# A decoder layer on one core: the middle piece's second copy moved to GpSimd, small columns batched, and the attention stage's orders rewritten

## What is computed

```python
# 1: self-attention, 16 heads of 8, rotary embedding on q and k
qkv = x @ w_qkv.T                       # per batch 128 x 384
q, k = rope(q), rope(k)
attn = softmax((q @ k.T) * 8 ** -0.5)   # 16 heads x 128 x 128 per batch
x = layernorm(x + (attn @ v) @ w_out.T + b_out)

# 2: cross layer over ctx: correlation by FFT, top 11 lags over all batches
q, k_, v = x @ Wq + bq, ctx @ Wq + bq, ctx @ Wq + bq      # 8 columns each
corr = real(ifft(fft(q) * conj(fft(k_)))).mean((0, 1))    # needs every batch
W, I = top_k(corr, 11); W = softmax(W)
R = sum(W[i] * roll(v, -I[i])); x = layernorm(x + tile(R) @ Wout + bout)

# 3: mixture of 8 experts, top 2, width 256, then two layer norms
y = mixed_experts(x) + x
x = layernorm(x + gamma * (y - mu) * rsqrt(var + 1e-5) + beta)
```

## Time and profile before

| what | us |
|---|---|
| median of 3 runs | 231.09 (230.35 to 231.51) |
| the profiled execution's own time | 231.02 |
| its span, first to last instruction | 229.2 |
| attention stage, about | 103 of the span |
| one batch in the steady part of that stage | 5.0 |
| TensorE busy | 214.5 |
| VectorE busy | 180.9 |
| ScalarE busy | 142.5 |
| GpSimd busy | 111.2 |

### The profile page before, as it was taken

One profiled execution on the slowest core, in us unless ns is written; L12 is line 12 of the kernel. 1 busy time (PEld: TensorE's weight loads), 2 busy tenths in 40 slices (PEclk: granted clock), 3 DMA queues, 4 the chain that ended last, 5 costly groups with the idle time before them and its releaser, 6 DMA issues.

```text
span 229.2 us, 7213 instructions
## 1 busy us (share of the span) xinstructions
PE 214.5 (94%) x2724; PEld 184.1 (80%) x2724; DVE 180.9 (79%) x622; ACT 142.5 (62%) x248; POOL 111.2 (49%) x219
## 2 busy tenths in 40 slices
PE   7989899999999979999999999999999999999970
PEld 7766677787777667778887999789988999889970
DVE  0588999999899899876755779897798868875885
ACT  2487899999999995674489300991029610596112
POOL 5189879999989995513630400252002600040484
PEclk9999999999999999999999999999999999999997
DMA  5951634665655651420000000001000100001001
GB/s 138 286 134 35 106 59 65 158 135 106 149 122 91 43 92 18 127 74 1 3 0 0 3 0 1 0 4 45 4 0 0 46 3 1 0 4 46 1 16 34
DMA packets 32454, 12.32 MB, mean 54 GB/s; under 512 B 19906, under 2 KB 32290, under 8 KB 32418
## 3 DMA queue, kind: packets, MB, share of 16 engines
q1 hardware_dynamic: 31554, 11.48, 24.1%
q10 hardware_dynamic: 864, 0.36, 0.7%
HBM read 6.33 MB, written 1.05 MB: 32 GB/s over the span
## 4 chain that ended last, share of the span: by engine, by line
PE 79%; DMA 7%; DVE 6%; ACT 3%; issue 2%; SPq 1%; DVEq 0%; ACTq 0%
PE bank L1328 13%; PE scoreT_pair L1328 12%; PE score_pair L1298 11%; PE scoreT_pair L1298 8%; PE bank L1042 6%; PE bank L1046 5%; PE bank L965 4%; PE scoreT_pair L997 4%; PE score_pair L981 3%; DMA qT_all<-mT 2%; PE bank L1003 2%; PE bank L1059 2%; DMA early<-in_ctxT 2%; DMA qT_all<-stack 2%; PE scoreT_pair L945 2%
## 5 line engine op out<-in xcount | busy, mean ns | idle before, releaser
L1385 DVE TENSOR_REDUCE rowmax<-score_pair 128x8 f32<-128x1024 f32 x32 | 39.0, 1218 | 4.4 <-PE score_pair L981 3.5
L608 POOL TENSOR_TENSOR ve<-mv,table 128x4 f32<-128x4 f32 (+1 forms) x12 | 3.3, 275 | 78.1 <-DVE mv L1745 60.2
L737 ACT ACTIVATE early<-scoreT_pair 128x1024 f32<-128x1024 f32 x32 | 32.8, 1026 | 6.3 <-PE scoreT_pair L997 6.1
L1328 PE MATMUL bank<-w,early 128*128 128x128 f32 x256 | 30.1, 276 | 0.0
L1328 PE MATMUL scoreT_pair<-w,early 128*128 128x128 f32 x256 | 29.9, 275 | 0.0
L1328 PEld LDWEIGHTS bank<-w,early 128*128 128x128 f32 x256 | 29.5, 192 | 0.3
L1328 PEld LDWEIGHTS scoreT_pair<-w,early 128*128 128x128 f32 x256 | 29.2, 192 | 0.0
L1298 PE MATMUL score_pair<-x2T_part,w_part 128*128 128x512 f32 x108 | 28.4, 398 | 0.0
L880 ACT ACTIVATE early<-score_pair,b 128x512 f32<-128x512 f32 x38 | 25.9, 690 | 3.2 <-PE score_pair L1298 2.6
L1042 PE MATMUL bank<-early,v_pad 128*32 128x128 f32 x512 | 26.5, 279 | 0.4 <-DVE attnT L1401 0.3
L1046 PE MATMUL bank<-early,head_ones 128*32 128x128 f32 x512 | 25.8, 273 | 0.0
(11 more groups left out here) (229 smaller groups left out, 472.3 us busy)
## 6 DMA issues: line engine op xcount, KB each, us to landing
w<-in_w SPq DMA_DIRECT2D x8, 256.0 KB, 3.7
x_ext<-in_x SPq DMA_DIRECT2D x4, 256.0 KB, 5.6
qT_all<-mT SPq DMA_DIRECT2D x32, 32.0 KB, 2.3
early<-in_xT SPq DMA_DIRECT2D x3, 256.0 KB, 4.8
early<-in_ctxT SPq DMA_DIRECT2D x3, 256.0 KB, 5.4
out<-qkv_all SPq DMA_DIRECT2D x3, 256.0 KB, 2.3
table<-in_tables SPq DMA_DIRECT2D x1, 321.0 KB
qT_all<-stack SPq DMA_TRANSPOSE x13, 3.3
```

What stands on the lines that cost most here:

```text
L737: act.activation(prob[n % 2][:, 2 * u:2 * u + 2, :, :], scoreT_pair[:, :].rearrange("p (i j s) -> p i j s", i=2, j=QUAD), ACT.Exp, scale=S ...
L1328: mm = pe.matmul(expert_bank[k % 4][:, e4 * D:(e4 + 1) * D], hT[:, f, n * P:(n + 1) * P], w2[:, f, :], start=(c == 0), stop=(c == CH - 1))
L1385: dve.tensor_reduce(rowmax[:, H // 2 * u:H // 2 * (u + 1)], score_pair[:, :].rearrange("p (r t) -> p r t", t=S), AX_X, ALU.max).then_inc(s ...
```

## The change

It touches the attention stage alone.

```diff
-        mv1 = [sb(f"mv1{i}", [P, 2]) for i in range(DEEP)]
-        ve1 = sb("ve1", [P, 1])
-        rs1 = [sb(f"rs1{i}", [P, 1]) for i in range(DEEP)]
+        mv1_all = sb("mv1_all", [P, DEEP, 2])
+        mv1 = [mv1_all[:, i, :] for i in range(DEEP)]
+        ve1 = sb("ve1", [P, 2])
+        rs1_all = sb("rs1_all", [P, DEEP])
+        rs1 = [rs1_all[:, i:i + 1] for i in range(DEEP)]
...
-            def inverse_deviation(n):
...
+            def inverse_deviations(n, end):
+
+                at, wide = n % DEEP, end - n
+                pool.wait_ge(s["y1_aggr"], end)
                 wait(pool, s["rs1_ready"], n)
...
+                pool.tensor_tensor(ve1[:, 0:wide], mv1_all[:, at:at + wide, 1], tab("eps")[:, 0:wide], ALU.add).then_inc(s["ve1_ready"], wide)
+                pool.wait_ge(s["ve1_ready"], end)
+                wait(pool, s["x1_ready"], end - DEEP)
+                pool.tensor_tensor(rs1_all[:, at:at + wide], ve1[:, 0:wide], tab("minus_half")[:, 0:wide], ALU.pow)\
+                    .then_inc(s["rs1_ready"], wide)
+
+            def second_copy(n):
+                pool.wait_ge(s["rest_ready"], n + 1)
+                pool.tensor_copy(piece(n, 5 * HD, 5 * HD), heads(rest[:, :])).then_inc(s["mid_copy"], 1)
...
+                pool.wait_ge(s["qkv_kept"], GT * (g + 1))
+                at = slice(GT * g, GT * (g + 1))
+                pool.tensor_tensor(x_ext[:, at, D:D + 2 * XC], qkv_all[:, at, 3 * D:QKV], small_b[:, :].unsqueeze(1).broadcast_to([P, GT, 2 * XC]),
+                                   ALU.add).then_inc(s["xe_ready"], 1)
```

In TensorE's list the two transposes thus move from behind `weighted` to behind the first `scores`, and in ScalarE's `mT_copy(6)` to `mT_copy(10)` stand behind the first exponential instead of ahead of it. Start and end of the lists, cut:

```diff
             qkv(0)
             keep_clock(3)
+            keep_clock(3)
             qkv(1)
-            keep_clock(3)
             turn_projection()
+            qkv(2)
             keep_clock(2)
-            qkv(2)
             keep_clock(2)
             qkv(3)
             q_transposes(0)
+            fold_cross_query()
             k_transposes(0)
...
+            keep_turned()
             third_piece(dve, 0)
+            remainder(dve, 1)
             residual(0)
-            remainder(dve, 1)
             qT_copy(0)
-            keep_turned()
             third_piece(dve, 1)
+            keep_folded()
             maxima(0, 0)
...
-            keep_clock(2)
-            scoresT(0, 0)
             scores(2, 0)
             maxima_transpose(1)
+            scoresT(0, 0)
             k_transposes(3)
             scoresT(0, 1)
             scores(2, 1)
             weighted(0, 0)
             weighted(0, 1)
+            scores(3, 0)
+            scoresT(1, 0)
+            maxima_transpose(2)
             k_transposes(4)
-            maxima_transpose(2)
-            scoresT(1, 0)
-            scores(3, 0)
             qkv(7)
```

More of the change, by code:

```diff
@@ new lines, in _ @@
+            project(1)
+            scoresT(2, 1)
+            scores(4, 1)
+            weighted(2, 0)
+            weighted(2, 1)
+            scores(5, 0)
+            scoresT(3, 0)
+            maxima_transpose(4)
+            k_transposes(6)
+            qkv(9)
+            scoresT(3, 1)
+            scores(5, 1)
+            project(2)
+            weighted(3, 0)
+            weighted(3, 1)
+            scores(6, 0)
+            scoresT(4, 0)
+            maxima_transpose(5)
+            k_transposes(7)
@@ new lines, in _ @@
+            qkv(10)
+            scoresT(4, 1)
+            scores(6, 1)
+            project(3)
+            weighted(4, 0)
+            weighted(4, 1)
+            scoresT(5, 0)
+            scores(7, 0)
+            maxima_transpose(6)
+            k_transposes(8)
+            qkv(11)
+            project(4)
+            scoresT(5, 1)
+            scores(7, 1)
+            weighted(5, 0)
+            weighted(5, 1)
+            scoresT(6, 0)
+            scores(8, 0)
+            maxima_transpose(7)
@@ new lines, in _ @@
+            k_transposes(9)
+            qkv(12)
+            project(5)
+            scoresT(6, 1)
+            scores(8, 1)
+            weighted(6, 0)
+            weighted(6, 1)
+            scoresT(7, 0)
+            scores(9, 0)
+            maxima_transpose(8)
+            k_transposes(10)
+            qkv(13)
+            project(6)
+            scoresT(7, 1)
+            scores(9, 1)
+            weighted(7, 0)
+            weighted(7, 1)
+            scoresT(8, 0)
+            scores(10, 0)
@@ L1172, in _ @@
+            k_transposes(11)
+            maxima_transpose(9)
+            qkv(14)
+            project(7)
+            scoresT(8, 1)
+            scores(10, 1)
+            weighted(8, 0)
+            weighted(8, 1)
+            scoresT(9, 0)
+            scores(11, 0)
+            k_transposes(12)
+            maxima_transpose(10)
+            qkv(15)
+            scoresT(9, 1)
+            scores(11, 1)
+            project(8)
+            weighted(9, 0)
+            weighted(9, 1)
             scoresT(10, 0)
+            maxima_transpose(11)
@@ new lines, in _ @@
+            statistics_of_rows(1)
+            pieces_of_maxima(dve, 4)
+            mean_and_variance(1)
+            reciprocal(2)
+            maxima(5, 0)
+            divide(2)
+            residual(3)
+            maxima(5, 1)
+            pieces_of_maxima(dve, 5)
+            residual_sum(2)
+            reciprocal(3)
+            maxima(6, 0)
+            divide(3)
+            normal_rows(dve, 0)
+            maxima(6, 1)
+            statistics_of_rows(2)
+            normal_rows(dve, 1)
@@ new lines, in _ @@
+            residual_sum(5)
+            maxima(8, 1)
+            pieces_of_maxima(dve, 8)
+            reciprocal(6)
+            statistics_of_rows(5)
+            divide(6)
+            maxima(9, 0)
+            residual_sum(6)
+            maxima(9, 1)
+            mean_and_variance(5)
+            pieces_of_maxima(dve, 9)
+            reciprocal(7)
+            divide(7)
+            maxima(10, 0)
+            normal_rows(dve, 3)
+            statistics_of_rows(6)
+            maxima(10, 1)
```

343 lines of the change are left out of this document (218 added, 125 removed).

## The result

The changed kernel takes 234.94 us (median of 20 runs, 232.33 to 237.52); the kernel before took 231.7 beside it (20 runs, 230.35 to 233.75). The ratio is 1.0099, with a 95% interval of 1.0069 to 1.0129: slower by 1%, outside the range that I gave. Ratios here compare means and leave out executions more than 1.5% above the fastest of their kernel (seven of these twenty, the profiled one among them), so they can differ from the quotient of the medians, which is 1.014. The profiled execution took 235.92, one of the longer ones; that of before took 231.02.

The account below looks back on a forecast made before the run. TensorE was taken to set the 5.0 us steady batch. Terms -0.8 (steady order), +0.5 (maxima), -0.5 (opening) and -0.8 (closing) sum to -1.6 from 231.02, forecasting 229.4 us; own range 228.6 to 229.9, whole range 227.1 to 232.0.

Parts of the forecast that it names:

- The maxima's way: Steady part: later copy delays the maxima's DMAs, so transposed scores of batches 6 to 8 wait; +0.5 us.
- t + 5.14 and t + 5.44: Next transposed scores' starts with landings of 2.8 and 3.1 us, t being this batch's start; turn due at t + 4.91.
- the waits move: Rival: maxima late in full (+1.0), closing wins nothing because VectorE's reciprocals come next; 230.7 us, chance 0.22.
- Steady order on TensorE: Maxima's transpose directly ahead of k's transposes saves 0.09 us a batch over nine batches; -0.8 us.
- Opening: Attention stage's start: the third batch's product comes earlier, less a longer way behind the first transposed scores; -0.5 us.
- Closing: Attention stage's end: TensorE's waits for an exponential and the last k copy go, turned q's stays; -0.8 us.
- GpSimd and ScalarE: Steady part: second copies leave ScalarE, GpSimd's batch grows from 4.65 to 4.70 us, below TensorE's; no cost.
- GpSimd as the bound: Rival: costlier copies or stretched operations make GpSimd's batch 5.23 us and transposes later; 232.5 us, chance 0.18.
- Interference: VectorE and GpSimd stretching each other: few encounters before, all off the path, so order wins little; 0.

Follow-up runs that it names:

- experiment 5: Changed kernel with the maxima's copy on ScalarE, transposes on TensorE and two pieces on VectorE moved early again; 231.63 us, ratio 1.0008.
- experiment 6: Same early maxima order as experiment 5, also without the changed kernel's added clock-keeping group; 231.49 us, ratio 0.9979.
- experiment 11: As experiment 6, but maxima's transposes early only in batches 5 to 10 and last activation load split over two SyncE turns; 231.30 us, ratio 0.9983.
- experiment 12: As experiment 11, but the maxima's transposes back behind the first scores pair on TensorE, where the change puts them; 233.04 us, ratio 1.0059.
- experiment 1: Changed kernel without the added clock-keeping group ahead of the second qkv; 234.44 us, ratio 1.0101.
- experiment 3: Changed kernel with the copy of the maxima's transposes ahead of the exponential on ScalarE in batches 5 to 9; 232.88 us, ratio 1.0054.
- experiment 10: Kernel before with only the four high parts of w1 spread on ScalarE as the change spreads them; 232.35 us, ratio 1.0029.
- experiment 2: Changed kernel with the second copies of batches 2 to 15 back on ScalarE; 234.58 us, ratio 1.0108.
- experiment 9: Kernel before with the second copies of batches 2 to 13 alone moved to GpSimd; 232.27 us, ratio 1.0014.
- Experiment 8: Kernel before with the second copies of batches 2 to 15 moved to GpSimd, else the old order; 239.12 us.

## Why the prediction was wrong

**The maxima's way, +0.5 between 0 and 1.0: this is the step that failed.** The mechanism and its place were right: the DMAs are issued 1.65 us behind the pair, to the hundredth as worked out. The size was not. The waits are 3.4 us in the five batches with the late copy (6 to 10), and batches 4 to 10 take 3.2 us more than before; experiments 5 and 6 take it back. First, I took the landings over from the trace before: the median, 2.3, or at most 3.1, behind the issue of the second DMA, that is 2.9 to 3.7 us from the first issue. The transfers of these batches took 3.44 to 4.46 from their first issue to the release of the pair, since most of the DMAs landed later than before (3.7 us in batch 10, where it was 2.4). Second, I let three batches be late, those with the long landings before; batches 9 and 10, with short ones before, waited 0.57 and 1.18. Third, "between nothing and 1.0 I take half" had no row behind it. The order leaves 4.91 - 1.65 = 3.26 us against 4.45 before, 1.2 us taken from each batch with the late copy, and that was the number to start from. There is a slip in the sum, too: t + 5.14 and t + 5.44 use 0.27 for the copy, where the text nets it to 0.2; by its own terms they are 5.07 and 5.37, and the waits 0.8 in sum and not 1.0. The sixth wait, 0.46 us in batch 5, I did not see at all. It comes from the load in front: in experiment 11, which splits that load, it is 0.18 us in place of 0.86.

The rival "the waits move" came nearest: late maxima and nothing won in the closing. It had the same wrong price for the first, and so ended at 230.7.

**Steady order on TensorE, -0.8: right as a price, wrong as a gain.** 4.91 was forecast, 4.87 to 4.93 measured up to batch 4. But the same edit takes its transpose from in front of the first pair to behind it, so what it saves it takes from the transfer. I costed the two as separate terms; by experiment 12 against 11 this one move costs some 1.7 us of the whole.

**Opening, -0.5: right in sign, larger (-1.08 from the second qkv on), and of little use** while the transfers set the pace: experiment 1 starts earlier and waits longer. The pair of batch 1, forecast near 27.5, starts at 29.72 in the stretched profile of the changed kernel, and at 27.65 and 27.56 in experiments 3 and 5, which have the same opening. The added clock-keeping group, which I had not priced, costs 0.66 us of TensorE by its rows (twelve products in 1.58 us in experiment 5, six in 0.91 or 0.92 in the kernel before), with no difference in time that the runs can tell.

**Closing, -0.8: not there.** The stretch took 29.43 against 29.52. Of the waits, the 0.25 for the exponential went as forecast, but the 0.52 for the last copy of k, which I let go too, is still 0.56 in the changed kernel; the 0.54 for the turned q, which I let stay, fell to 0.24. I named the reciprocals as next. In experiment 10, with the high parts of w1 spread and nothing else, the exponential and the copy of k are what TensorE waits for, and longer than before.

**GpSimd and ScalarE: right.** The copy measured 0.397 us by the median (0.40 forecast), and 0.86 at most, the pair of deviations about 0.70 (0.715), four batches' small columns 0.32 (0.31). In experiments 2 and 9 the copy is free either way, within some 0.4%. The rival that ended slower, GpSimd as the bound, had the right sign by a cause that does not hold: GpSimd waits for ScalarE 0.6 to 1.4 us in some batches of the changed kernel.

**Interference, 0: right for the changed kernel, and only for its order.** Experiment 8 is what I should have looked at as well: the copies of all fourteen batches in the old order come with a loss of 7.5 us. What the new GpSimd order is for can't be seen in a comparison of before and after alone.

## What to carry to other kernels

Where a transfer lies between two engines' lists, note the time it is given, from its issue to the operation that needs it, and not only its landing. An edit that takes some of that time away is priced against the whole way from first issue to release. A trace in which nobody waits bounds that way only from above (here by 4.45 us), and the landings in it need not stay when the order around them changes. Terms that touch the same recurrence are one term. When a list is lengthened on GpSimd, look for the short VectorE operation that will meet GpSimd's longest unbroken chain, above all where all of TensorE waits for it.

## What the runs showed of the hardware

A VectorE cast can be held while GpSimd's operations run: in most cases here until the one operation in which it began was over (0.65 to 1.07 us), once over a whole chain, where 0.22 us became 5.81. Behind TensorE's wait of 4.65 us for that the granted clock fell to 0.50, and the next two batches took 3.5 us more. A small case, VectorE's and GpSimd's rows of the changed kernel, where the normal rows (0.34 before) take 0.83 beside a third piece that keeps its 0.67:

```profile
73.58 0.83 DVE L471 TENSOR_SCALAR x_all<-y,mv_all,rs_all 128x136 f32<-128x136 f32 x1
```

```profile
73.65 0.67 POOL L458 TENSOR_TENSOR stack<-rest,stack 128x256 bf16<-128x256 f32 x1
```

In the opening of before it was GpSimd's third piece that was stretched; here it is VectorE's side. The other surprise is the first 10 us, where the same products took 0.94 to 1.49 us from one execution to the next. The granted clock of these stretches is given as 1.00 in the slow cases as in the fast ones, so the traces do not tell the cause.
